# A float32 output product rewritten as three rounded passes, with work moved around it, in an attention and expert kernel

## The reference, cut to what matters

```python
def attn(x, w_kv_down, w_kv_up, w_q, w_out):        # x: (8, 512, 128), 16 heads of 64
    kv = (x @ w_kv_down) @ w_kv_up
    k, v = heads(kv[..., :1024]), heads(kv[..., 1024:])
    q = heads(x @ w_q)
    att = softmax(causal(einsum('bqhd,bkhd->bhqk', q, k) * 64 ** -0.5))
    y = einsum('bhqk,bkhd->bqhd', att, v).reshape(8, 512, 1024)
    return y @ w_out
def ffn(x, Wr, Wg, Wu, Wd):                         # 8 experts of hidden size 512, top 2
    top_vals, top_idx = top_k(x @ Wr, 2)
    combine = weights(softmax(top_vals), top_idx)
    eo = einsum('neh,ehc->nec', silu(x Wg) * (x Wu), Wd) * 12 ** -0.5
    return einsum('ne,nec->nc', combine, eo)
x = x + attn(layernorm(x)); x = x + ffn(layernorm(x))
```

## Time and profile before

| | |
|---|---|
| median of 3 runs | 870.66 us (869.91 to 870.77) |
| the profiled execution | 868.56 us |
| its span, first to last instruction | 866.8 us |
| TensorE busy | 846.0 us, 98% |
| VectorE, ScalarE, GpSimd busy | 620.2, 625.7, 572.4 us |
| mean granted TensorE clock | 0.997 of full |

### The profile page before, as it was taken

How to read it: one execution, slowest core, us unless ns; L and a number is a source line. 1 busy time by engine, 2 the same in 40 slices (tenths; PEclk the granted TensorE clock), 3 DMA queues, 4 the chain that set the end, 5 groups by cost and what they waited for, 6 DMA issues and landing times.

```text
span 866.8 us, 20127 instructions
## 1 busy us (share of the span) xinstructions
PE 846.0 (98%) x6535; PEld 670.2 (77%) x6535; DVE 620.2 (72%) x2348; ACT 625.7 (72%) x1639; POOL 572.4 (66%) x522
## 2 busy tenths in 40 slices
PE   8999999999999999999999999999998999999995
PEld 4677777777777777777777777777767999988884
DVE  6677787887777777878778778788787665545442
ACT  5877777877787777778877778777796776555552
POOL 5475576578657956775787569666748667555664
PEclk9999999999999999999999999999999999999998
DMA  7575550000000000000000000000011344333342
GB/s 197 207 285 211 235 161 2 1 26 8 7 8 26 1 7 9 24 8 1 21 13 7 5 29 1 8 7 26 8 26 44 48 56 67 44 51 48 50 53 26
DMA packets 44038, 44.69 MB, mean 52 GB/s; under 512 B 4112, under 2 KB 36240, under 8 KB 43936
## 3 DMA queue, kind: packets, MB, share of 16 engines
q0 software_dynamic: 16528, 26.03, 12.4%
q1 hardware_dynamic: 27120, 17.25, 7.1%
q10 hardware_dynamic: 288, 0.13, 0.1%
HBM read 15.28 MB, written 28.12 MB: 50 GB/s over the span
## 4 chain that ended last, share of the span: by engine, by line
PE 88%; DVE 4%; POOL 3%; issue 2%; ACT 2%; POOLq 0%; DVEq 0%; ACTq 0%
PE low_ps L1322 12%; PE low_ps L1309 9%; PE mid_ps L1244 7%; PE mid_ps L1246 7%; PE mid_ps L1245 7%; PE out_ps L1333 7%; PE top_ps L1309 7%; PE mid_ps L1295 6%; PE low_ps L1295 4%; PE low_ps L1534 4%; PE top_ps L1295 4%; POOL prob L408 2%; DVE prob L847 2%; PE out_ps L1509 2%; PE top_ps L1244 2%; PE top_ps L1246 2%
## 5 line engine op out<-in xcount | busy, mean ns | idle before, releaser
L408 POOL TENSOR_TENSOR prob<-prob,row_inv 128x512 f32<-128x512 f32 (+3 forms) x256 | 318.7, 1264 | 200.2 <-DVE row_inv L854 199.8
L588 ACT ACTIVATE prob<-prob,neg_max 128x256 f32<-128x256 f32 (+3 forms) x512 | 280.6, 550 | 7.8 <-DVE neg_max L847 0.9
L1322 PE MATMUL low_ps<-PT,v_sb 128*64 128x512 f32 (+3 forms) x1024 | 152.0, 439 | 0.3 <-ACT PT L594 0.3
L1322 PEld LDWEIGHTS low_ps<-PT,v_sb 128*64 128x64 f32 x1024 | 68.1, 136 | 92.1 <-issue 65.2
L859 DVE COPY PT<-low_ps 128x512 f32<-128x512 f32 (+1 forms) x128 | 104.1, 814 | 16.0 <-PE low_ps L1309 13.5
L599 ACT ACTIVATE v_sb<-mid_ps 128x512 f32<-128x512 f32 x64 | 38.3, 598 | 94.0 <-PE mid_ps L1246 93.8
L1160 DVE TENSOR_TENSOR prob<-mid_ps,prob 128x512 f32<-128x512 f32 x71 | 49.0, 691 | 78.1 <-PE mid_ps L1246 43.9
L847 DVE CUSTOM_DVE_ANT_0 prob<-mid_ps,mask 128x128 f32<-128x128 f32 (+1 forms) x256 | 93.5, 421 | 9.1 <-PE mid_ps L1295 4.9
L1309 PE MATMUL low_ps<-ident,prob 128*128 128x128 f32 x640 | 94.5, 278 | 2.0 <-POOL prob L408 0.5
L588 ACT ACTIVATION_READ_ACCUMULATOR prob<-prob,neg_max 128x1 f32 x512 | 95.7, 187 | 0.0
L594 ACT ACTIVATE PT<-top_ps 128x1024 f32<-128x1024 f32 x64 | 65.7, 1026 | 37.8 <-PE top_ps L1309 32.5
(11 more groups left out here) (253 smaller groups left out, 1872.2 us busy)
## 6 DMA issues: line engine op xcount, KB each, us to landing
routed_rows<-W_dn POOLq DMA_DIRECT2D x8, 2080.0 KB
X<-routed_rows SPq DMA_DIRECT2D x37, 65.0 KB
X<-routed_rows SPq DMA_DIRECT2D x17, 130.0 KB
X<-in_L_attn_x SPq DMA_DIRECT2D x8, 256.0 KB, 5.3
W_ffn<-in_L_ffn_Wg SPq DMA_DIRECT2D x8, 256.0 KB, 4.4
W_ffn<-in_L_ffn_Wu SPq DMA_DIRECT2D x8, 256.0 KB, 4.6
W_dn<-in_L_ffn_Wd SPq DMA_DIRECT2D x8, 256.0 KB, 4.7
out<-X SPq DMA_DIRECT2D x8, 256.0 KB, 2.3
```

The costliest lines, as they stand in the source:

```text
L408: nc.gpsimd.tensor_tensor(p_pair(i), p_pair(i), row_inv[:, i, :].unsqueeze(2).to_broadcast([P, 2, P * (i + 1)]), ALU.mult).then_inc(S["nor ...
L588: nc.scalar.activation(p_at(i, h), p_at(i, h), ACT.Exp, bias=neg_max[:, i, h:h + 1], scale=-1.0, accum_out=row_sum[:, i, h:h + 1]).then_in ...
L1322: last = nc.tensor.matmul(y_ps[h * HD:(h + 1) * HD, j * P:T], v_sb[:, half, j, o + h * HD:o + (h + 1) * HD], PT[:, h, j, j:NT, :].rearrang ...
```

## The change

The output product becomes three rounded passes. The output weight is split once, in step 0, into a high and a low part in `Wo_sb[:, 2, NP, C]`. y gets a high part (ScalarE's `y_copy`, now float32r) and a low part (`y_lo`, a new VectorE subtraction in each step, ahead of the last reciprocal and of tile 1's copy). The weight is now stationary and y moves, 512 columns wide, so `out_ps` holds the result with channels on the partitions: ScalarE copies it out once a batch (`post_out`, k=8), TensorE transposes it back in four blocks (`post_out`, k=1), and `post_x2` reads the result of that, in k=2 where it was k=1.

Around it, the order changes. ScalarE copies y between the two exponentials of tile 3. VectorE takes the reciprocal of tiles 1 and 0 between the two heads' maxima of tiles 2 and 3. `post_choose` moves behind the copies of k=5, in front of `post_chosen`; `pre_stats` behind the copies of k=1; `split_lo` behind the copies, and that of expert 0 from step 62 to behind tile 1's copy of step 63. The cast of `row_i` moves from `post_weights` (k=7) to `post_rows` (k=6), and ScalarE's `post_gap` from k=5 to k=6. At the end of step 63, y's copy goes ahead of the Silu table's load, and y's low part ahead of the splits of experts 2 and 6. Small buffers share the space of others.

```diff
-        Wo_sb = sb("Wo_sb", [P, NP, C])
+        Wo_sb = sb("Wo_sb", [P, 2, NP, C], F32R)
...
-        y_sb = sb("y_sb", [P, T])
+        y_sb = sb("y_sb", [P, T], F32R)
...
+        y_parts = [y_sb[:, :].rearrange("p (a n) -> p a n", a=2), xT_sb[:, 0, :, :]]
+        outT = xn2T
...
-        SPLIT_LO = {STEPS - 20: [1], STEPS - 12: [5], STEPS - 2: [0]}
+        SPLIT_LO = {STEPS - 20: [1], STEPS - 12: [5]}
...  # ScalarE
                 if cur:
                     exps(n, 2)
-                    exps(n, 3)
+                    exp_head(n, 3, 0)
                 y_copy(n - 1)
+                if cur:
+                    exp_head(n, 3, 1)
...
-                if post is not None and k == 5:
+                if post is not None and k == 6:
                     post_gap(post)
-                if post is not None and k == 6:
                     post_second(post)
...
+                if k == NP:
+                    post_out(n // NP - 1)
                 if cur:
                     t3_copy(n)
...
+            def post_out(b):
+                seen(act, S["out_ready"], NP * (b + 1))
+                seen(act, S["logits_ready"], b)
+                nc.scalar.activation(outT[:, :], out_ps[:, :], ACT.Copy).then_inc(S["outT_copied"], 1)
...
             w_hi(Wv, 1, post_ps[:, :])
+            act.wait_ge(wo_in, 16)
+            nc.scalar.activation(Wo_sb[:, 0, :, :], Wo_in, ACT.Copy).then_inc(S["wo_hi"], 1)
...
                 if j == 0:
+                    post_out(B - 1)
                     split_hi(7)
...
             split_hi(3)
+            y_copy(STEPS - 1)
             nc.scalar.activation(gap_exp[:, 0:1], eps[:, 0:1], ACT.Silu)
-            y_copy(STEPS - 1)
...  # VectorE
+            def y_lo(n):
+                seen(dve, S["y_copied"], n + 1)
+                seen(dve, S["out_ready"], n)
+                nc.vector.tensor_tensor(y_parts[1], y_ps.rearrange("p (a n) -> p a n", a=2), y_parts[0].bitcast(F32),
+                                        ALU.subtract).then_inc(S["y_lo_done"], 1)
...
-                    maxes(n, 2)
+                    max_head(n, 2, 0)
                     inv(n, 1)
-                    maxes(n, 3)
+                    max_head(n, 2, 1)
+                    max_head(n, 3, 0)
                     inv(n, 0)
+                    max_head(n, 3, 1)
                     inv(n, 2)
-                for e in SPLIT_LO.get(n, []):
-                    split_lo(e)
-                if post is not None and k == 1:
+                if post is not None and k == 2:
                     post_x2(post)
-                if pre is not None and k == 1:
-                    pre_stats(pre)
...
-                if post is not None and k == 5:
-                    post_choose(post)
                 if post is not None and k == 7:
                     post_weights(post)
+                y_lo(n - 1)
                 if cur:
                     inv(n, 3)
                     t_copy(n, 1)
+                if n == STEPS - 1:
+                    split_lo(0)
                 if nxt:
                     qk_lo(n + 1)
                 if cur:
                     t_copy(n, 2)
                     t_copy(n, 0)
+                for e in SPLIT_LO.get(n, []):
+                    split_lo(e)
...
+                if pre is not None and k == 1:
+                    pre_stats(pre)
...
                 if post is not None and k == 5:
+                    post_choose(post)
                     post_chosen(post)
...
-            for i in (2, 0):
-                t_copy(0, i)
+            t_copy(0, 2)
+            dve.wait_ge(S["wo_hi"], 1)
+            nc.vector.tensor_tensor(Wo_sb[:, 1, :, :], Wo_in, Wo_sb[:, 0, :, :].bitcast(F32), ALU.subtract)\
+                .then_inc(S["wo_lo"], 1)
+            t_copy(0, 0)
...
                 if j == 0:
-                    post_x2(B - 1)
                     split_lo(3)
                 if j == 1:
+                    post_x2(B - 1)
                     post_stats(B - 1)
...
-            for e in (4, 2, 6):
+            split_lo(4)
+            y_lo(STEPS - 1)
+            for e in (2, 6):
                 split_lo(e)
...  # TensorE
             def project_out(n, pair):
-                seen(pe, S["y_copied"], n + 1)
+                seen(pe, S["y_lo_done"], n + 1)
                 if pair == 0:
-                    seen(pe, S["x2_done"], n // NP)
+                    seen(pe, S["outT_copied"], n // NP)
+                for k, (w, part) in enumerate(((0, 0), (1, 0), (0, 1))):
+                    last = nc.tensor.matmul(out_ps[:, :].rearrange("p (a n) -> p a n", a=2), Wo_sb[:, w, pair, :], y_parts[part],
+                                            start=(pair + k == 0), stop=(pair == NP - 1 and k == 2), skip_group_check=True)
+                last.then_inc(S["out_ready"], 1)
+            def post_out(b):
+                seen(pe, S["outT_copied"], b + 1)
+                if b < B - 1:
+                    seen(pe, S["routing"], ROUTING * (b - 1) + 14)
                 for t in range(NT):
-                    last = nc.tensor.matmul(out_ps[:, t * P:(t + 1) * P], y_sb[:, t * P:(t + 1) * P], Wo_sb[:, pair, :],
-                                            start=(pair + t == 0), stop=(pair == NP - 1), skip_group_check=True)
-                last.then_inc(S["out_ready"], 1)
+                    last = nc.tensor.transpose(post_bank(b)[:, t * P:(t + 1) * P], outT[:, t * P:(t + 1) * P], ident[:, :])
+                last.then_inc(S["outT_ready"], 1)
```

More of the change, by code:

```diff
@@ L177, in layer @@
         hT_sb = [PT[:, a, 0, :, :].rearrange("p i q -> p (i q)") for a in range(2)]
-        eo_sb = [o[:, q * C:(q + 1) * C] for o in (prob[:, 4 * T:5 * T], y_sb) for q in range(RING)]
+        eo_sb = [o[:, q * C:(q + 1) * C] for o in (prob[:, 4 * T:5 * T], v_sb[:, 0, 0, :]) for q in range(RING)]
         w_up_sb = W_ffn[:, 0:2, :].rearrange("p a n -> p (a n)")
@@ L841, in maxes, with max_head @@
             def maxes(n, i):
-                seen(dve, S[f"t{i}_ready"], n)
-                w = P * (i + 1)
-                seen(dve, S["s_ready"], NT * n + max(POS[i], POS[2] if i == 0 else 0) + 1)
-                for h in range(2):
-                    nc.vector.tensor_tensor_reduce(out=p_at(i, h), in0=scores_at(i, h), in1=mask[:, T - w:T],
-                                                   scale=-SCALE, scalar=BIG, op0=ALU.add, op1=ALU.min,
-                                                   accum_out=neg_max[:, i, h:h + 1]).then_inc(S["max_done"], 1)
+                for h in range(2):
+                    max_head(n, i, h)
+            def max_head(n, i, h):
+                if h == 0:
+                    seen(dve, S[f"t{i}_ready"], n)
+                    seen(dve, S["s_ready"], NT * n + max(POS[i], POS[2] if i == 0 else 0) + 1)
+                w = P * (i + 1)
+                nc.vector.tensor_tensor_reduce(out=p_at(i, h), in0=scores_at(i, h), in1=mask[:, T - w:T],
+                                               scale=-SCALE, scalar=BIG, op0=ALU.add, op1=ALU.min,
+                                               accum_out=neg_max[:, i, h:h + 1]).then_inc(S["max_done"], 1)
             def inv(n, i):
@@ L1018, in post_x2 @@
             def post_x2(b):
-                seen(dve, S["out_ready"], NP * (b + 1))
+                seen(dve, S["outT_ready"], b + 1)
                 xs = X[:, 4 * b:4 * b + 4, :].rearrange("p a c -> p (a c)")
-                nc.vector.tensor_tensor(xs, out_ps[:, :], xs, ALU.add).then_inc(S["x2_done"], 1)
+                nc.vector.tensor_tensor(xs, post_bank(b), xs, ALU.add).then_inc(S["x2_done"], 1)
             def post_stats(b):
@@ L1375, in post_xn2T @@
                 seen(pe, S["xn2_done"], 4 * b + 4)
+                seen(pe, S["x2_done"], b + 1)
                 if b == B - 2:
@@ L1518, in wide_down @@
                 if j == 2:
-                    seen(pe, S["x2_done"], B)
+                    seen(pe, S["outT_copied"], B)
                 for c in range(2):
```

37 lines of the change are left out of this document (24 added, 13 removed).

## The result

The changed kernel takes 873.21 us (median of 7 runs, 871.87 to 874.43) beside 870.31 us for the kernel before (7 runs on the same chip, 869.52 to 871.02): a ratio of 1.0034, with a 95% interval of 1.0023 to 1.0046. It is a little slower. Measured again later, beside other kernels, it was 1.0069 (1.0046 to 1.0092). One of the twelve executions of a later kernel, turn_as_before, took 1667 us where the others took 871 to 874, and is left out of that kernel's ratio.

What follows compares the result with a forecast made beforehand. TensorE bounds the kernel before; plain steps then become bound by ScalarE and VectorE. First batch -1.2, middle 0, steps 57-62 -0.15, step 63 +1.2, turn +1.85: +1.7 gives 870.3, plus 2.1 to the median, 872.4 us; range 866 to 877.

Steps and rivals of the forecast that it cites:

- one sign of being wrong: Plain steps of 9.7 and more with the last reciprocal behind y's subtraction would mean slower than forecast.
- The output product: TensorE's product in each step: 0.95 us before, then 0.69 after the projection or 0.78 after transposes; TensorE alone 9.53.
- The added wait and the chain: Plain steps: y's low part just covered; last reciprocal and tile 1's copy delay tile 2's transposes to S+7.04-7.10; step 9.61.
- The choice: Moved to k=5's end, with one-hot rows 2.05 us; next first maximum 1.0 late, k=6 10.59 against 9.96.
- The rival that waits would pay for the choice: Choice at the step's end paid by waits the chain keeps anyway: 869 us at half cost, 865.5 at none; chance 0.27.
- k=7: Row cast moved from k=7's free middle to k=6's end makes k=7 0.17 longer: 9.78, no gain.
- Step 63: Expert 0's split, moved here, slows GpSimd's last norm: +0.96, with 0.24 for the late start +1.2 us.
- The turn: Attention to experts: table load behind y's copy, two splits behind y's low part; first gate product 3.6 after values, +1.85.
- The experts: Experts' part after the turn, bound by TensorE, gives nothing back.
- it is faster: Rival, chance 0.27: TensorE stays the bound, waits pay for the choice; 869 or 865.5 us; decides below 0.45 a batch.
- The chain is longer in every step: Rival, chance 0.20: exposed weight load or y's subtraction ending S+6.3 or later; 0.1 in about 45 steps, 877 us.
- The turn is hidden: Rival, chance 0.20: split meets the middle norm, or VectorE's waits in experts' first turns absorb the delay; -2 us, 870.4.

Runs made afterwards that it cites:

- turn_as_before: Changed kernel with the turn's old order: Silu table load ahead of y's copy, VectorE's three splits ahead of y's low part; ratio 1.0001.
- y_lo_behind_copy: Changed kernel with y's low part behind the last reciprocal and VectorE's copy of tile 1 in every step; 942.91 us, one run.
- choice_mid: Changed kernel with the choice back in the middle of k=5, ahead of y's low part; ratio 1.0044.
- gap_late: Changed kernel with the choice back in the middle of k=5, except its subtraction of the two best, put at the step's end; ratio 0.9968.
- weights_on_act: Changed kernel without VectorE's last product of the weights; ScalarE writes that value as it copies the columns; ratio 0.9993.
- weight_one_input: Changed kernel with the second routing weight in k=7 made from one SBUF input (DEPTH_SCALE minus the first), not two; ratio 1.0019.
- all_three: Changed kernel with last weight product on ScalarE, choice in mid k=5 with its subtraction at the end, and the turn's old order; 863.57 us, ratio 0.9961.
- recip_pairs: Changed kernel with only the reciprocals put back behind both heads' maxima, as in the kernel before; ratio 1.0035.
- product_only: Changed kernel keeping the three-pass product, with choice, reciprocals, input statistics, expert 0's split and the turn put back; ratio 0.9986.
- the halves: Two runs of the changed kernel, each keeping only one engine's changed order at the turn; ratios 1.0041 (VectorE's kept) and 1.0063 (ScalarE's kept).
- turn_vector_only: Changed kernel with ScalarE's order at the turn as before (table load ahead of y's copy), VectorE's as changed; ratio 1.0041.
- turn_scalar_only: Changed kernel with VectorE's order at the turn as before (three splits ahead of y's low part), ScalarE's as changed; ratio 1.0063.
- changed_again: The changed kernel itself, unedited, measured again beside other kernels in the third group; 871.65 us, ratio 1.0069.

## Why the prediction was right, and where its terms were not

The forecast was 872.4 us, and 873.2 was measured. In medians the change costs 2.9 us where the sum said 1.7; between the two profiled executions it is 5.1, and when both kernels were measured again it was 4.1. That the forecast came within 0.8 us is in part luck, since its errors had both signs. In a middle batch k=2, 5, 7 and 8 came out 0.56 above the forecast together and k=1, 3, 4 and 6 came out 0.44 below; step 63 was priced 0.9 too high, and the first batch gained 0.26 less than forecast. Of the signs named beforehand, most came, but the last norm of step 63 took 1.90 and not 2.9, and one sign of being wrong came too: plain steps of 9.7 with the last reciprocal right behind y's subtraction (312.63 behind 312.61). The terms, one by one.

*The output product* was sized about rightly. Behind transposes it takes 0.78 from its first pass to the next transposes, as forecast (k=1, S+6.66 to S+7.44); k=4 falls by 0.19 (forecast 0.11). In the plain step the third pass starts 0.52 after the first, where 0.46 was assumed, and with 0.24 behind the third pass, as in k=1, the product takes 0.77 there and not 0.69. That alone brings TensorE's own bound from 9.53 to 9.61. The four transposes ahead of the product in k=1 and k=3 cost 0.35 (S+6.31 to S+6.66), not 0.44, which is why these two steps were forecast too high.

*The added wait and the chain.* y's copy S+4.91 (forecast 4.92), low part S+5.52 (5.53), tile 1's copy S+6.31 (6.32): each within 0.01. Tile 2's transposes start at S+7.13, not at 7.04 to 7.10, and 2.57 lie from there to the next step, not 2.53. So a plain step is 9.70 and not 9.61. The term was small and the step frequent: k=2, 5 and 8 are each 0.08 to 0.09 above the forecast. What the transposes wait for is tile 1's copy: in k=2, 5, 6 and 8 of the changed kernel they start 0.15 us behind its end, in k=6 too, where the copy ends 0.75 later than in k=5. But the margin is small. The product by itself would let them start at about S+7.08, 0.05 earlier, and y_lo_behind_copy shows that it has no more slack than 0.06. So chain and TensorE bound the plain step almost together, and "no longer by TensorE" in the prediction was too strong.

*The choice* was the right place and near the right size: k=6 10.44 against 10.59, its first maximum 0.73 late against 1.0. I had put 1.31 and 0.71 together at 2.05 (they make 2.02); it took 1.98 (315.69 to 317.68), and began 0.05 early. choice_mid and gap_late both give back 0.66 to 0.69. The rival that waits would pay for the choice is ruled out by the same number.

*k=7* is where the prediction's working failed: "The row cast ... makes k=7 0.17 longer: 9.78". The cast did no harm. What happened is that the reciprocals between the heads bring GpSimd's norms forward, tile 2's norm onto the weights' last operation, and that VectorE operation is held until the norm ends. Wherever the held operation stands, it ends with the norm: 1.18 and 1.19 us (weights) and 1.15 (the choice's subtraction) at tile 2's norm, 0.27 and 0.23 at tile 0's. With the operation gone (weights_on_act) the step is 9.69. I had noted in the prediction that the reciprocals move the norms by 0.45, and costed only GpSimd's side.

The hold could have been read from the trace of the kernel before. There the choice's subtraction and the cast of `row_i` meet tile 0's norm. The first takes 0.23 and ends at 311.98, the norm at 311.96. The second takes 0.39 and ends at 331.72, where that step's norm ends at 331.70; the same cast takes 0.17 in k=6 of the changed kernel. VectorE and GpSimd of the kernel before:

```profile
311.75 0.23 DVE L1060 TENSOR_TENSOR gap<-top 128x4 f32<-128x4 f32 x1
...
331.33 0.39 DVE L1096 CAST row_i<-row_f 128x8 int32<-128x8 f32 x1
```

```profile
311.35 0.61 POOL L408 TENSOR_TENSOR prob<-prob,row_inv 128x256 f32<-128x256 f32 x1 [0.24 <-DVE row_inv L854]
```

The Trainium skill, SBUF — State Buffer, section SBUF: two separate sides, states this as a rule: a VectorE instruction with two SBUF inputs or in a two-port mode and a GpSimd instruction take one pair of ports as an exclusive lock, and whichever starts second waits for the whole of the first. The traces here agree with it in both directions, and weight_one_input (held with one input) fits its second case. The prediction used the Trainium skill, GPSIMD Engine Reference, section Specifications, which says only that the two contend, and read it as a slowdown of GpSimd alone.

*Step 63.* The same error with the other sign. The prediction let the split of expert 0 lengthen the last norm: +0.96, with the late start +1.2. The norm started first, kept its 1.90 and was not late for its transposes; the split waited. What step 63 costs is 15.19 - 14.89 = 0.30 us, as turn_as_before beside the kernel before shows, and it is not the split's: step 63 is a k=7, and weights_on_act, without the held product, gets 0.37 back in it. all_three keeps the split in step 63 and has 14.82. recip_pairs keeps it too and has 16.69, which is 14.87 without the turn's 1.82, and product_only with the split back in step 62 has 14.89. So the split's new place costs nothing that can be seen.

*The turn.* Forecast +1.85, measured 17.01 - 15.19 = +1.82. The working named table and splits together; the halves show that VectorE's two splits make the whole of it and that the table load, moved alone, would cost 0.94. The price of 2.66 us for a table switch, which the prediction set beside it from the Trainium skill, ScalarE: Activation LUTs, section What ACT_TABLE_LOAD costs, is not seen: the load takes 1.28 and the next activation starts at once.

*The experts.* "It gives nothing back": true, but it took 2.1 us more in the profiled execution. In all fourteen profiles the time from h(0) to the end lies between 203.5 and 209.9 us (204.2 in the kernel before), and the changed kernel has 206.3 and 203.5 in its two. So this difference isn't charged to the change. One part of it can be named. VectorE's sum for the last batch's x, moved behind slot 1, waits although TensorE's transposes for it ended at 667.98 (VectorE, then windows, of the changed kernel):

```profile
668.89 0.15 DVE L1197 SCALAR_TENSOR_TENSOR wdT<-X,pad_row 128x2 int32<-128x2 f32 x1
...
670.36 0.69 DVE L1062 TENSOR_TENSOR X<-low_ps,X 128x512 f32<-128x512 f32 x1 [1.31 <-remote]
```

```profile
672.00:676.00 4.00, 2.12 (x14) 2.12 (x15) 3.24 (x10) 0.00 (x0) 1.72 (x3) 0.89 0.23 66
676.00:680.00 4.00, 4.00 (x26) 3.86 (x25) 2.54 (x10) 3.27 (x6) 3.18 (x2) 0.68 0.18 16
```

"Remote" is a releaser that the trace does not name. TensorE idles 2.70 us behind this, and then its clock falls. The wait of 1.1 to 1.5 us is in the profiles of seven kernels (the changed one, choice_mid, weight_one_input, recip_pairs, weights_on_act, turn_vector_only, product_only) and absent in gap_late, turn_as_before, turn_scalar_only, y_lo_behind_copy, all_three and changed_again; since the same program has it once and once not, it hangs on the moment and not on the code alone. What releases it stays open.

Of the rivals, "it is faster" was ruled out by the choice's price, which was above the 0.45 us from which it would decide. "The chain is longer in every step" was right in kind and nearly in size: 0.09 in each plain step where it said 0.1, but not for its reasons, since y's subtraction ended at S+6.21 and the last reciprocal was on time. "The turn is hidden" did not happen, the turn cost 1.8. In all, the choice cost 7 x 0.66 us, the turn 1.8, the hold 6 x 0.39 and 0.37 in step 63, some 9.2 together; all_three has 9.7 less than changed_again in its steps 9 to 62 and the turn (at the turn reckoned against 17.01), and 8.1 in the medians. What the change gained against these is the lower plain step, the stall of k=8, 1 and 2, and the first batch, -0.94 against -1.2 forecast. So the answer to where the gain went: with most moves undone the change gains about 1.2 us (product_only, 0.9986, 0.9976 to 0.9995), which is no more than the unexplained difference between weight_one_input and the changed kernel; with the reciprocals between the heads and the repairs the ratio is 0.9961 (all_three). Two moves and one side effect took it back.

## What to carry to other kernels

Where VectorE and GpSimd both work on SBUF, read each short VectorE operation against the GpSimd intervals of the new schedule: a product of four columns costs what is left of the norm it meets, and moving a reciprocal, which is itself free, can put the two on top of each other. Split a bookkeeping block before moving it: most of the choice could stay in its wait, and only its one operation that is held had to leave. When two engines' orders are changed at one transition, try each alone, since side by side only the longer delay counts and the shorter one is invisible until the other is mended.

## What the runs showed of the hardware that I had not expected

- A VectorE TENSOR_TENSOR or TENSOR_SCALAR of four float32 columns from SBUF to SBUF, issued during a GpSimd operation on SBUF, ends 0.02 to 0.03 us after that operation, at 1.15 to 1.19 us instead of 0.15. A CAST of eight columns does the same (0.39 instead of 0.17 at the short norm). RECIPROCAL (0.18), FIND_INDEX8 (0.16), and operations with PSUM as a source (MAX8, copies, y's low part at 0.69) issued during the same norms keep their durations.
- The other way round, a GpSimd operation on one column (L429, 0.19 otherwise) took 1.18 us beside a VectorE split that had begun to run.
- TensorE's granted clock fell in step 63 behind 1.7 us of idle time in changed_again (a mean of 0.61 from 656 to 660 us) and in gap_late, and stayed at 1.00 behind the same idle time in the first profile of the changed kernel. Six transposes then take 1.49 us instead of 0.82, and h(0) comes 1.45 later.
- The changed kernel's ratio to the kernel before was 1.0034 (1.0023 to 1.0046) once and 1.0069 (1.0046 to 1.0092) later, and the kernel before had medians of 871.06 and 867.57 us in two groups on one chip. Two kernels with the same steps and the same turn, weight_one_input and turn_vector_only, have 1.0019 and 1.0041. Ratios that should agree thus differ by 0.2 to 0.35%, to the edge of their intervals; steps read from the traces are the safer ground.
